# A graph network's message stage: TensorE's side jobs moved behind each chunk's sums, and its placements spread 2, 2 and 6 over three steps

## The reference, cut to what matters

```
for l in range(4):
    e = edge_attr @ We[l] + be[l]                      # rank 1: weight of the edge times a row
    m = relu(x[src] + e)                               # 40,000 messages of 512
    agg = segment_sum(m, dst)                          # 1250 x 512
    h = ((1 + eps[l]) * x + agg) @ W1[l] + b1[l]
    h = relu((h - mean(h)) * rsqrt(var(h) + 1e-5) * gamma[l] + beta[l])
    x = relu(h @ W2[l] + b2[l])
```

## Time and profile before

| | |
|---|---|
| median of three runs | 1772.68 us |
| profiled execution, its span | 1772.85 us, 1771.1 us |
| PE, busy | 1462.0 us, 83% |
| DVE, busy | 1310.3 us, 74% |
| POOL, busy | 1081.7 us, 61% |
| ACT, busy | 944.5 us, 53% |
| mean granted clock of TensorE | 0.942 |
| the dense stage of layers 1, 2 and 3 starts on TensorE at | 858.85, 1233.12 and 1607.15 us |

### The profile page before, as it was taken

The page is one execution under the profiler, slowest core; times in us unless marked ns, Lnnn a source line. Parts: engine busy times, 40 slices in busy tenths (PEclk is TensorE's granted clock), DMA queues, the critical chain, the costliest instruction groups (busy, mean ns, idle before and its releaser), DMA issues.

```text
span 1771.1 us, 22116 instructions
## 1 busy us (share of the span) xinstructions
PE 1462.0 (83%) x6948; PEld 645.9 (36%) x6948; DVE 1310.3 (74%) x2539; ACT 944.5 (53%) x1086; POOL 1081.7 (61%) x1070
## 2 busy tenths in 40 slices
PE   3767898867787888888888988889888898898797
PEld 2233344322333333333433333334433333334464
DVE  6788988978457887776586778776678878685634
ACT  3544544444245666665436667665456666673221
POOL 3777777777126777777047777773267777770033
PEclk8988999887999999999999999999999999999889
DMA  7776677677147777776257777783477777866343
GB/s 261 204 201 188 196 199 200 197 225 226 51 125 221 216 212 212 210 213 199 53 179 228 223 228 212 215 233 111 141 225 221 224 217 210 244 196 230 149 149 111
DMA packets 119094, 343.23 MB, mean 194 GB/s; under 512 B 20712, under 2 KB 24892, under 8 KB 118718
## 3 DMA queue, kind: packets, MB, share of 16 engines
q0 software_dynamic: 85248, 278.41, 55.0%
q1 hardware_dynamic: 32318, 60.78, 10.6%
q10 hardware_dynamic: 1408, 2.56, 0.4%
HBM read 323.61 MB, written 19.96 MB: 194 GB/s over the span
## 4 chain that ended last, share of the span: by engine, by line
PE 45%; DVE 16%; POOL 13%; ACT 12%; issue 8%; DMA 4%; DVEq 1%; POOLq 0%; ACTq 0%; SPq 0%
PE ps L1799 41%; POOL ring L817 13%; ACT ring L1593 10%; DVE ring L1006 8%; PE ps L1864 3%; DMA ring<-x_table,idxT 3%; DVE lg L1061 1%; DVE aggT L1421 1%; DVE onehot L1000 1%; DMA aggT<-pair_table,token_i 1%; DMA ring<-in_x 1%; DVEq L1048 0%; PE ps L2229 0%; DVE ring L940 0%; DVE aggT L1062 0%
## 5 line engine op out<-in xcount | busy, mean ns | idle before, releaser
L817 POOL DMA_INDIRECT ring<-x_table,idxT x1014 | 1039.3, 1025 | 514.4 <-issue 293.1
L1006 DVE SCALAR_TENSOR_TENSOR ring<-we_bc,wT,ring 128x512 f32<-128x512 f32 x1014 | 688.7, 747 | 63.6 <-DMA ring<-x_table,idxT 58.5
L1593 ACT ACTIVATE ring<-ring 128x3072 f32<-128x3072 f32 x161 | 444.7, 2762 | 282.9 <-DVE ring L1006 282.9
L1799 PE MATMUL ps<-ring,onehot 128*32 128x512 f32 x2028 | 360.2, 650 | 198.3 <-ACT ring L1593 194.5
L1639 ACT ACTIVATE zT<-ps 128x512 f32<-128x512 f32 x336 | 189.6, 601 | 145.6 <-PE ps L1799 142.7
L1799 PE MATMUL ps<-ring,zT 128*128 128x512 bf16 x1080 | 262.4, 382 | 0.8
L1799 PE MATMUL ps<-zT,xT 128*32 128x512 f32 (+2 forms) x752 | 256.5, 618 | 1.6 <-DVE mix L1195 1.6
L1061 DVE TENSOR_REDUCE lg<-ps 128x128 f32<-128x512 f32 x208 | 143.1, 688 | 118.0 <-PE ps L1864 72.2
L1799 PEld LDWEIGHTS ps<-ring,onehot 128*32 128x32 f32 x2028 | 72.3, 113 | 381.5 <-ACT ring L1593 242.9
L1799 PE MATMUL ps<-w,zT 128*125 128x512 f32 (+2 forms) x320 | 146.5, 621 | 20.2 <-ACT zT L1717 20.2
L1799 PE MATMUL ps<-aggT,w 128*128 128x512 f32 (+1 forms) x384 | 142.7, 522 | 6.9 <-DVE aggT L1062 3.6
(11 more groups left out here) (311 smaller groups left out, 1263.2 us busy)
## 6 DMA issues: line engine op xcount, KB each, us to landing
ring<-x_table,idxT POOLq DMA_INDIRECT x1014, 3.8
zT<-slot_table SPq DMA_DIRECT2D x36, 312.5 KB
w<-in_L_gnn_W SPq DMA_DIRECT2D x8, 1024.0 KB, 10.7
ring<-in_L_ffn_W SPq DMA_DIRECT2D x16, 512.0 KB, 9.8
x_table<-ring SPq DMA_DIRECT2D x24, 250.0 KB
x_table<-ring SPq DMA_DIRECT2D x9, 256.0 KB
stage<-in_x ACTq DMA_DIRECT2D x9, 256.0 KB
pair_table<-mix SPq DMA_DIRECT2D x9, 256.0 KB
```

The costliest lines, as they stand in the source:

```text
L817: gp.indirect_dma_start(out=to, out_offset=None, in_=table[:, :], in_offset=bass.IndirectOffsetOnAxis(ap=idx, axis=0)).then_inc(done, 16)
L1006: ins = v.scalar_tensor_tensor(out=at[:, u, :], in0=we_bc[:, :], scalar=wT[:, c, u:u + 1], in1=at[:, u, :], op0=ALU.mult, op1=ALU.add)
L1593: a.activation(at, at, ACT.Relu).then_inc(relu_done, 1)
L1799: return nc.tensor.matmul(o, lhsT, rhs, start=start, stop=stop)
```

## The change

On TensorE, in layers 1 to 3, a step's order is now: first picked tiles, the chunk's sums, placements, the fold of the chunk before, the fold of a picked chunk, later picked tiles, and behind them the side job and the early sums. The flush of a picked chunk moves to the step after, and so do VectorE's and ScalarE's parts of the side jobs (`beside_of`). Placements are 2, 2 and 6 over the three steps of a picked chunk in place of 3, 4 and 3, with other row groups (`LATER_LANE`). In step 38 the fold of chunk 37 and of the last picked chunk stand between the first and second pair, and early sums before the third. Early sums from the fifth quarter on wait also for the last picked chunk's copy. Layer 0 keeps its order.

```diff
@@ -142,13 +142,13 @@
 
 
     def placed_at(l, j):
-        first, later = tiles_of(l, j - 1) if j > 1 else ([], [])
-        return first + later
+        q, m = (j + 1) // 3, (j + 1) % 3
+        return [] if j < 2 or q >= NQ else list(range(q * SW + (0, 2, 4)[m], q * SW + (2, 4, 10)[m]))
 
     LANE = [(s % G, s < G, s + G >= SW) for s in range(SW)]
-    LATER_LANE = [(2, True, False), (3, True, False), (0, True, False),
-                  (2, False, False), (3, False, False), (0, False, False), (1, True, True),
-                  (2, False, True), (3, False, True), (0, False, True)]
+    LATER_LANE = [(2, True, False), (3, True, False),
+                  (2, False, False), (3, False, False),
+                  (2, False, False), (3, False, False), (0, True, True), (1, True, True), (2, False, True), (3, False, True)]
 
 
     def copy_at(j):
@@ -161,6 +161,10 @@
         if j == 1:
             return 0
         return (j - 2) // 3 if j % 3 == 2 and 5 <= j <= 3 * NQ - 1 else None
+
+    def beside_of(l, j):
+
+        return beside_at(l, j - 1)
 
 
 
@@ -189,8 +193,8 @@
         for j in range(NJ[l] + 2):
             if 0 <= j - 2 < NJ[l]:
                 order.append(("j", j - 2))
-            if l in MIXED and fold_at(j) is not None:
-                order.append(("q", fold_at(j)))
+            if l in MIXED and fold_at(j - 1) is not None:
+                order.append(("q", fold_at(j - 1)))
         assert len(order) == NC
         ORDER.append({o: i for i, o in enumerate(order)})
 
@@ -1031,16 +1035,21 @@
                 for p in range(PAIRS):
                     v.wait_ge(last_got[f][p], (l + 1) * PAIR * 16)
                     add_tiles(l, j, range(p * PAIR, (p + 1) * PAIR)).then_inc(last_summed, 1)
-                    if f == FINE - 1 and p == 1:
+                    if l in MIXED:
+                        if p == 0:
+                            flush(l, "j", j - 2)
+                            if f > 0:
+                                early_stats(l, early_of(l, j - 1))
+                        if p == 1:
+                            flush_picked(l, j)
+                            early_stats(l, early_of(l, j if f > 0 else j - 1))
+                    elif f > 0 and p == 1:
                         flush(l, "j", j - 2)
-                        if l in MIXED:
-                            early_stats(l, early_of(l, j))
                 if f == FINE - 1:
                     flush(l, "j", j - 1)
                     flush(l, "j", j)
-                else:
+                elif l not in MIXED:
                     flush(l, "j", j - 2)
-                    flush_picked(l, j)
 
             def flush(l, kind, i):
 
@@ -1063,8 +1072,8 @@
 
             def flush_picked(l, j):
 
-                if l in MIXED and fold_at(j) is not None:
-                    flush(l, "q", fold_at(j))
+                if l in MIXED and fold_at(j - 1) is not None:
+                    flush(l, "q", fold_at(j - 1))
 
             def early_stats(l, e):
 
@@ -1108,13 +1117,10 @@
                     else:
                         add_fine(l, j)
                     beside(l, j)
-                    if l in MIXED:
-                        if ready_at(j) is not None:
-                            picked_ready(l, ready_at(j))
-                        if j < NJ[l] - 1:
-                            early_stats(l, early_of(l, j))
-                    else:
+                    if fine_of(l, j) is None or l not in MIXED:
                         early_stats(l, early_of(l, j - 1))
+                    if l in MIXED and ready_at(j) is not None:
+                        picked_ready(l, ready_at(j))
 
             def general(l):
                 left = v.value_load(left_i[0:1, 0:1], min_val=0, max_val=1)
@@ -1183,7 +1189,7 @@
                 return n0[0]
 
             def beside(l, j):
-                for kind, i in dve_jobs[j - 1] if l == 0 else beside_at(l, j):
+                for kind, i in dve_jobs[j - 1] if l == 0 else beside_of(l, j):
                     job(l, kind, i)
 
             def job(l, kind, i):
@@ -1608,15 +1614,16 @@
                     a.wait_ge(last_summed, (l * FINE + f) * PAIRS + p + 1)
                     q = slice(p * PAIR, (p + 1) * PAIR)
                     a.activation(slots[:, k, q, :], slots[:, k, q, :], ACT.Relu).then_inc(last_relu, 1)
-                    if f > 0 and p == 0:
+                    if p == 0 and (f > 0 or l in MIXED):
                         parts_copy(l, j - 1)
-                        if l in MIXED:
-                            early_copy(l, early_of(l, j - 1))
-                parts_copy(l, j if f > 0 else j - 1)
-                if l in MIXED and f == 0:
-                    early_copy(l, early_of(l, j - 1))
-                if l in MIXED and f > 0:
-                    early_copy(l, early_of(l, j))
+                    if l in MIXED and f > 0 and p == 1:
+                        early_copy(l, early_of(l, j - 1))
+                if f > 0:
+                    parts_copy(l, j)
+                elif l not in MIXED:
+                    parts_copy(l, j - 1)
+                if l in MIXED:
+                    early_copy(l, early_of(l, j if f > 0 else j - 1))
 
             def early_copy(l, e):
 
@@ -1718,7 +1725,7 @@
                                      bias=sc[:, 4, fo:fo + 1], scale=sc[:, 3, fo:fo + 1]).then_inc(z_ready, 1)
 
             def beside(l, j):
-                for kind, i in act_jobs[j - 1] if l == 0 else beside_at(l, j):
+                for kind, i in act_jobs[j - 1] if l == 0 else beside_of(l, j):
                     if kind == "columns":
 
                         if i > 0:
@@ -1846,13 +1853,22 @@
                 for p in range(PAIRS):
                     if f > 0 and p == PAIRS - 1:
                         fold_groups(l, j - 1)
+                    if l in MIXED and f == 0 and p == 1:
+                        fold_groups(l, j - 1)
+                        if fold_at(j) is not None:
+                            fold_picked(l, fold_at(j))
+                    if l in MIXED and f == 0 and p == PAIRS - 1:
+                        early_sums(l, early_of(l, j))
                     pe.wait_ge(last_relu, (l * FINE + f) * PAIRS + p + 1)
                     for u in range(p * PAIR, (p + 1) * PAIR):
                         g = u % G
                         ins = mm(ps[b][g * WIN:(g + 1) * WIN, :], onehot[:, k, u, :],
                                  slots[:, k, u, :], u < G, u + G >= U)
                 ins.then_inc(parts_done, 1)
-                fold_groups(l, j if f > 0 else j - 1)
+                if f > 0:
+                    fold_groups(l, j)
+                elif l not in MIXED:
+                    fold_groups(l, j - 1)
 
             def fold_groups(l, j):
 
@@ -1893,6 +1909,7 @@
                     picked_added(l, min(x for x in EARLY_MIXED if EARLY_MIXED[x] == e))
                 elif l in MIXED:
                     pe.wait_ge(pick_relu, QB[l + 1] * SW)
+                    pe.wait_ge(pick_out, QB[l + 1])
                 elif e >= KD:
                     pe.wait_ge(h_copied, early_before(l) + e - KD + 1)
                 first_layer(l, e // KD, e % KD, early_bank(l, e)).then_inc(h_done, 1)
@@ -1957,26 +1974,33 @@
                             place_rows(l, T)
                 group_sums(l, 0)
                 for j in range(1, NJ[l]):
+                    if l not in MIXED:
+                        beside(l, j)
+                        early_sums(l, early_of(l, j))
+                        if fine_of(l, j) is not None:
+                            fine_sums(l, j)
+                        else:
+                            group_sums(l, j)
+                            fold_groups(l, j - 1)
+                        continue
+                    if fine_of(l, j) is not None:
+                        if fine_of(l, j) > 0:
+                            early_sums(l, early_of(l, j))
+                        fine_sums(l, j)
+                        continue
+                    first, later = tiles_of(l, j)
+                    for T in first:
+                        take_rows(l, T)
+                    group_sums(l, j)
+                    for T in placed_at(l, j):
+                        place_rows(l, T)
+                    fold_groups(l, j - 1)
+                    if fold_at(j) is not None:
+                        fold_picked(l, fold_at(j))
+                    for T in later:
+                        take_rows(l, T)
                     beside(l, j)
                     early_sums(l, early_of(l, j))
-                    if fine_of(l, j) is not None:
-                        if l in MIXED and fold_at(j) is not None:
-                            fold_picked(l, fold_at(j))
-                        fine_sums(l, j)
-                        continue
-                    first, later = tiles_of(l, j) if l in MIXED else ([], [])
-                    for T in first:
-                        take_rows(l, T)
```

(10 more changed lines are left out.)

## The result

The changed kernel took 1784.77 us (median of 9 runs, 1777.63 to 1787.93) against 1773.23 of the kernel before (9 runs); the ratio is 1.0064 (95% interval 1.0045 to 1.0084). The range ended at 1783, the forecast was 1775.3. The profiled execution of the changed kernel took 1777.63 us (span 1775.9), its lowest of the nine, 4.8 us above before's profiled 1772.85. So two things are to be explained: the 4.8 us between the two traces, and some 7 more that the median has and this trace has not. Ratios here compare executions within 1.5% of the fastest of their kernel, so that they can differ from the quotient of two medians.

The account below looks back on a forecast made before the run. GpSimd's gathers were taken to bound layers 1 to 3. Layer 1 at -1.7, layer 2 at +2.2 and layer 3 at +2.1 us gave +2.6 on 1772.7, so 1775.3 us; range 1764 to 1783.

Parts of the forecast that it names:

- GpSimd's gathers set the pace, the middle is worth 0: Layers 1 to 3 between head and tail: gathers set the pace, reordering gains 0, bound -2 to +4 us per layer.
- The lanes: Placed tiles on TensorE: two of three steps save a 0.85 us wave, 61 us in all, nearly all hidden beside gathers.
- The head, -0.5 us in layers 2 and 3: Start of layers 2 and 3: the picked fold now follows step 1's sums, saving 0.5 us each; layer 1 gains 0.
- The tail, sums(37): End of layers 1 to 3: sums(37) can start 10.9 us after chunk 37's last gather, moving by -6.2, -1.8, -1.9 us.
- The tail, what follows: From sums(37) to the dense stage: 24.4 us instead of 19.9, +4.5 us per layer.
- The clock: TensorE's granted clock in the tails: named as what could spoil them, as more waits per step lie ahead; priced in rival 1.
- the dense stages are untouched: Dense stages after the layers: taken as unchanged by the change, together with layer 0 and the experts.
- Rival 1: Tails of layers 1 to 3: waits for landings drop TensorE's clock to 0.90, +8 us in all, 1783 us; chance 0.22.

Follow-up runs that it names:

- e15: Kernel before with the sixth gather of chunks 5 to 37 left out in layers 1 to 3, usual chip; 1755.50 us, ratio 0.9912.
- e16: Changed kernel with the sixth gather of chunks 5 to 37 left out in layers 1 to 3, usual chip; 1744.77 us, ratio 0.9855 to the full kernel before.
- e4: Changed kernel's order without its lanes, placements 3, 4, 3 as in the kernel before; 1793.91 us, ratio 1.0139.
- e3: Kernel before with only the change's lanes and 2, 2, 6 placements, old order; 1772.09 us, ratio 1.0007.
- e1: Changed kernel run again whole, with a second profile; 1785.40 us against 1772.09 for the kernel before, ratio 1.0082.
- e2: Changed kernel with the last steps undone: fifth early sum ahead of sums(37), steps 38 and 39 in the old order; 1775.04 us, ratio 1.0014.
- e6: Changed kernel with six idle 512-column matmuls per layer in TensorE's last waits before the dense stage, on a slow chip; ratio 0.9990 to the kernel before.
- e11: Changed kernel with six idle 512-column matmuls per layer in TensorE's last waits before the dense stage, usual chip; 1783.80 us, ratio 1.0062.
- e12: e10 plus idle 512-column matmuls (two, one, two per layer) in the last waits before the dense stage; 1770.38 us, ratio 0.9986.
- e13: e10 plus short idle 256-column matmuls (two, one, three per layer) in the last waits; 1765.98 us against 1771.46 for the kernel before, ratio 0.9965.
- e17: Changed kernel plus short idle 256-column matmuls (three, one, three per layer) in the last waits, slow chip; 2016.48 us against 2008.37 before, ratio 1.0061.
- e10: Changed kernel up to step 34, the order of the kernel before from step 35 on, new lanes throughout; 1771.20 us against 1770.89, ratio 1.0004.
- e7: Kernel before with the sixth gather of chunks 5 to 37 left out in layers 1 to 3, on a slow chip (2016 us before); ratio 0.9343.
- e18: Changed kernel itself with a third profile, on a slow chip; 2027.17 us against 2008.37 for the kernel before, ratio 1.0076.

## Why the prediction was wrong, step by step

- **GpSimd's gathers set the pace, the middle is worth 0:** right. Chunks 5 to 37 take 260 to 264 us in every profile with six gathers on a usual chip, whatever the order. What the text did not see is how thin the cover is: 0.4 to 0.6 us per chunk (e15, e16), and none in layer 1 when the order comes without the lanes (e4).
- **The lanes:** TensorE's busy time fell by 42 us rather than 61 (27 with the lanes alone, e3), hidden as said; but in layers 2 and 3 they alone bring sums(37) to 10.6 to 10.8 us (e3).
- **The head, -0.5 us in layers 2 and 3:** too small to see. From the dense start to chunk 5 layer 2 took 79.91 us for 80.51, within the 1.9 us over which clean ends scatter; layer 3 took 81.13 for 79.18, behind a half-rate end.
- **The tail, sums(37):** right, 11.0, 10.7 and 10.6 us for a predicted 10.9.
- **The tail, what follows:** +4.5 was mis-sized, it is 25.4 - 19.9 = +5.5 in clean layers. A lone pair costs 0.98, not 0.85 us, an early sum 3.6 with its gap, and the last pair's relu is waited for 1.61 us instead of 0.88. (The terms that the prediction lists for the new order also add up to 17.4 and not 17.5.) With that the sum is 36.36 + 36.1 + 36.0 - 102.3 = +6.2, not +2.6.
- **The clock, and "the dense stages are untouched":** this is the step that failed. The prediction put the start of the dense stages at nothing; seven of nine ends of the changed kernel were half-rate there, none of six before. A half-rate end makes the 32 matmuls 1.6 to 2.6 us longer, which is most of the 2.2 us that it costs up to the next chunk 5; a late start costs 2.3 more. Three ends of 2.2 us, seven times of nine, are about +5; with the tails' +6.2 and a late start now and then that is 11 to 14 us, an estimate from these figures, against 11.5 and 13.3 by the medians. Rival 1 (0.22) had the direction and nearly the size (1783), but that closeness is luck: it had the whole tails at 0.90, on top of +2.6. Of the changed kernel's six tails on usual chips one had such a half-rate stretch (layer 2 in e1, 1.6 us); else they ran at full rate until their last microseconds.
- **What is shown of it:** undoing the last steps returns 10 of 13 us (e2), and the half-rate starts go when the last waits are filled (e6, e11, e12, e13, e17). By time this is shown only on the kernel with the old last steps, between e10 (1.0004) and e13 (0.9965). The idle matmuls remove half-rate ends and late starts together, so these runs don't part the two, nor whether one brings the other. The Trainium skill (TensorE: Matmul & The Clock Gate, "HAM oscillation — how this bites in real kernels") says that a matmul loop which waits for its DMAs falls back to the slow clock and pays for it after each wait. The traces agree as to direction: the half rate stands behind waits here (for relus, copies and flushes, not for DMAs) and goes when they are filled; but the kernel before has nearly the same waits and was clean six times of six. In the middle the clock fell too (0.96 for 1.00) and cost nothing, since the gathers covered it.

**Left open:** why the ends are half-rate in the changed kernels and not in the one before. Before's last waits are 0.88, 0.70 and 1.22 us; in e10 they are the same, in e3 too but for one late start, and two of three ends were half-rate. Both halves of the change bring it (e3, e4), and the kernel before with five gathers had it too (e15, one of three; e7, two). So these waits alone don't decide it, and no run here found what does. Open too is why TensorE starts late for its own issue. Nor has e17 shown by time alone that the changed kernel's surplus goes.

## What to carry to other kernels

Work moved behind a stage's last input is paid in full, even where the same move is free in every step before: treat the last steps of a loop apart, as e13 does, and count the waves and gaps that a split group costs. Before you value a gain in the middle of a loop, ask how far the next limit is; here it was 0.4 to 0.6 us per chunk of 7.9, and even that was under cover. What a change puts at nothing, here the stage behind the loop, deserves a row of its own in the next trace. Where the last waits of a stage stand ahead of a block of dense matmuls, look at the granted clock in that place in several profiles; a few short matmuls into a free bank, sized by the waits, held it in e13.

## What the hardware showed unexpectedly

- A mean clock can fall without cost: e3 has TensorE at 0.927 of full rate on average over its executions where before has 0.942, at the same time (1.0007). What counts is where the half rate falls.
- An idle f32 matmul 128x128x512 is recorded as two instructions and takes 0.9 us; with 256 columns 0.45. Six long ones per layer cost 1.4 us of each tail (e11), six short ones nothing (19.92 us in e13 and e10).
- Four of six sets of runs fell on chips where before takes 1771 to 1773 us, two on chips at 2008 and 2016. TensorE stood for its own issue 160 us (87 times) in e18, and GpSimd's gathers, still 1.3 us apart in a row, waited for the ring (129.5 us); the answer to one question differed: five gathers saved the kernel before 6.6% there and 0.9% here, and with them the changed kernel was the slower there and the faster here.
